# Opening of a fused FFN, attention, FFN kernel: third chunk's sums in two more banks, masks stored a chunk sooner; squares ahead of weights and routing a slot later in the attention phases

## The chip, the cores and the metric

The kernel runs on one core of a Trainium2 chip. The metric is the device time of one execution in microseconds. The core has a matrix engine (TensorE, in the profile PE, with PEld for its weight loads), and VectorE (DVE), ScalarE (ACT) and GpSimd (POOL), which work between the on-chip memory (SBUF) and the accumulators (PSUM, eight banks of 128 x 512 fp32); SyncE (SP) issues DMAs here and computes nothing. ACT and POOL issue DMAs too. Each engine runs its own instructions in the order in which they are written, and they are tied to each other by semaphores.

## The reference, cut to what matters

```python
x = x + 0.5 * ffn(layernorm(x))      # x: 2048 tokens x 512, fp32
x = x + attention(layernorm(x))
x = x + 0.5 * ffn(layernorm(x))

def ffn(x):                          # 64 experts in 8 groups of 8
    scores = softmax(x @ gate_w.T)
    topk_w, topk_idx = top_k(scores, 8)
    w_e = zeros((N, 64)).at[arange(N)[:, None], topk_idx].add(topk_w)
    flat = w_e[:, inv_map]           # N x 8 groups x 8
    scalar = flat.sum(-1)
    soft = softmax(where(flat == 0, -1e9, flat))
    xg = x[:, None] + einsum('ngi,ghi->ngh', soft, mask_up_w)
    g = einsum('ngh,gih->ngi', xg, gate_proj_w)       # i: 352
    u = einsum('ngh,gih->ngi', xg, up_proj_w)
    d = einsum('ngi,ghi->ngh', silu(g) * u, down_proj_w)
    return einsum('ng,ngh->nh', scalar, d)

def attention(x):                    # 4 heads, chunks of 64 tokens
    q, k, v, g = x @ Wq, x @ Wk, x @ Wv, x @ Wg
    gk = log_sigmoid(x @ Wgk1 @ Wgk2 + b) / 16
    o = chunkwise gated linear attention(q, k, v, gk)
    return (rms(o) * Wnorm * silu(g)) @ Wo
```

## The kernel before

**Tiles and phases.** The tokens lie in four blocks of 512. A phase is the FFN of one block, so there are eight phases (`p`), four for each FFN. The 8 x 352 inner columns are cut into 22 chunks of 128 (`CH`; `n = 22 p + i` counts chunks over all phases). For each chunk PE does: the gate sums (`main`, 12 matmuls of 128x512 into a bank, since each fp32 product is three fp32r ones of high and low halves, helper `three`), the mixing matmul that adds the experts' mask part (`soft`, L1380), the same for the up sums, and later the down group of the chunk before (`down(n - 1)`, 12 matmuls into the four banks `YB`, which collect the phase's output). ACT takes silu of the gate bank (L682, `sig`), DVE multiplies by the up bank (L758, `act_t<-bank,sig`) and by the routing scalar (`s_bc`, loaded by ACT, L677), ACT rounds the product (`a_hi`, L509) and DVE subtracts the rest (`a_lo`). `GB`, `UB` are the gate and up bank, `W0`, `W1` two work banks (6 and 7); chunk 1 alone has its gate and up sums in `YB[0]` and `YB[1]`, which are still free.

**Weights.** Phase 0 makes them. SP loads raw weights, ACT casts the high half (`gu_hi`, `d_hi`, L509), DVE subtracts for the low half (`gu_lo`, `d_lo`), PE multiplies the masks with the gate and up weights (`masked(c)`, 8 half-width matmuls L1361, L1362 into `W0`), DVE picks the group's rows (`m_mask`), ACT and DVE round that (`m_top`, `m_rest`), and POOL stores all to DRAM (`store_w`, `store_m`, `store_d`). From phase 1 on SP loads each chunk's weights back: `load_w` (L309, 1152 KB, two buffers `wt`, waits for `u_ok` of two chunks before) and `load_d` (L318, 512 KB, `dt`).

**Slots.** The work between the FFN matmuls is cut into 66 slots for each phase, three for each chunk (`pieces(3 * n)`, `3 * n + 1`, `3 * n + 2`); every engine calls `pieces` at the same places. Phases 1, 2, 4 and 5 (`ATT`) carry the attention of one block each, in slots 13 to 65. All phases but the last carry the routing of the next phase's tokens: statistics, normalization, split of the normalized tokens into `x_hi` (ACT) and `x_lo` (DVE) in `split_slot(p)` and the slot after it, the logits on PE in slot 38 (`router(p, 38)`, L1205, waits for `x_lo_ok`), and the softmax, the top 8 and the transposes in slots up to 51. Before them SP and POOL turn the normalized tokens by quarters with sixteen DMAs of 64 KB (`move_squares`, eight on each queue; SP's are L333); the attention's own tokens are turned likewise at chunk 4 of its phase. In SP's program for chunk 4 the order is `load_w(p, 4)`, `move_squares`, `load_d(p, 3)`.

**The opening.** Ahead of the phase loop PE transposes and routes the first block, does the masks of chunks 0 and 1, the sums of chunks 0 and 1, the transposes of `scal` (L1218) and the eight of `route` (L1224, into `YB[2]` and `YB[3]`, four each). ACT copies these to `softT` (`route_cp`), and only then can the mixing matmuls run. `down(0)` comes in chunk 2's turn, since its banks `YB[0]` and `YB[1]` hold chunk 1's sums until then. ACT issues five DMAs of constants before it casts the weights of chunk 2 (`gu_hi(2)`), and DVE subtracts (`gu_lo(2)`) just before the phase loop.

## Time and profile before

| What | Value |
|---|---|
| Median of three runs | 1832.6 us (1831.39 to 1835.84) |
| The profiled execution | 1832.78 us, of it the span 1831.0 us |
| Mean granted TensorE clock | 0.998 |
| PE busy | 1811.0 us, 99% |
| PEld busy | 1507.7 us, 82% |
| DVE busy | 875.4 us, 48% |
| ACT busy | 512.6 us, 28% |
| POOL busy | 215.6 us, 12% |

How to read the rows. A timeline row has the start in us from the span's start, the duration, the engine, the line, the operation, out<-in, the shapes and how many instructions are taken together; in square brackets stands the engine's idle time just before, and what ended it. "ACTq" and "SPq" are DMA issues on ACT's and SP's queue. A row of a window has its bounds and length, then the busy time and number of instructions of PE, PEld, DVE, ACT, POOL and SP's, then PE's granted clock, the share of the DMA engines and GB/s. A row of DMAs has how many, KB of each, and us from issue to landing. Row numbers of lines are those of the kernel before.

### The profile page before, as it was taken

The numbers are of one execution on the slowest core, as the hardware profiler recorded it, in microseconds if no ns is written. First come the engines' busy times: TensorE is split into PE (matmuls) and PEld (weight loads), VectorE is DVE, ScalarE is ACT, GpSimd is POOL, SyncE is SP. The second block draws the span as 40 slices with busy tenths as digits, with TensorE's granted clock in tenths as the row PEclk, the third lists the DMA queues.
The fourth block names the chain that finished last, engine by engine and source line by source line (L and its number), as shares of the span: only waits on it lengthen the run. The fifth ranks groups of instructions, "written<-read, shape, count | busy, mean of one in ns | idle before, by whom it ended". The sixth has DMA issues, their size and how long they took to land.

```text
span 1831.0 us, 22143 instructions
## 1 busy us (share of the span) xinstructions
PE 1811.0 (99%) x8376; PEld 1507.7 (82%) x8376; DVE 875.4 (48%) x1621; ACT 512.6 (28%) x766; POOL 215.6 (12%) x390
## 2 busy tenths in 40 slices
PE   7999999999999999999999999999999999999999
PEld 5888888888888888888888888888888888888887
DVE  7567454565445663333353656354664334422222
ACT  4334313532125431112212533124432111211111
POOL 1141220011010210010110111010011001000000
PEclk9999999999999999999999999999999999999999
DMA  6987765456365555467756556474456367656664
GB/s 209 363 320 273 276 221 183 157 201 207 125 218 203 168 185 190 166 235 235 246 183 199 192 205 207 139 241 161 154 194 215 134 222 259 226 173 226 236 233 167
DMA packets 103657, 382.04 MB, mean 209 GB/s; under 512 B 16288, under 2 KB 20256, under 8 KB 82816
## 3 DMA queue, kind: packets, MB, share of 16 engines
q1 hardware_dynamic: 58768, 270.50, 42.3%
q0 software_dynamic: 16992, 62.93, 9.3%
q10 hardware_dynamic: 27792, 47.20, 9.2%
q8 instruction: 67, 1.10, 0.2%
q14 instruction: 38, 0.31, 0.1%
HBM read 323.55 MB, written 41.81 MB: 200 GB/s over the span
## 4 chain that ended last, share of the span: by engine, by line
PE 92%; DMA 2%; DVE 2%; issue 1%; ACT 1%; SPq 1%; POOL 0%; ACTq 0%; DVEq 0%; POOLq 0%
PE bank L1176 27%; PE bank L1178 27%; PE bank L1177 27%; PE bank L1380 4%; DMA x_lo<-tb 2%; SPq L333 1%; PE bank L1316 1%; PE bank L1315 1%; PE bank L1361 1%; PE bank L1362 1%; PE bank L1302 1%; PE bank L1308 1%; PE bank L1205 0%; DVE x_lo L758 0%; PE bank L1206 0%
## 5 line engine op out<-in xcount | busy, mean ns | idle before, releaser
L1176 PE MATMUL bank<-x_hi,wt 128*128 128x512 f32 x1328 | 521.2, 393 | 0.0
L1178 PE MATMUL bank<-x_lo,wt 128*128 128x512 f32 x1328 | 517.3, 390 | 0.0
L1177 PE MATMUL bank<-x_hi,wt 128*128 128x512 f32 x1328 | 516.8, 389 | 0.0
L758 DVE TENSOR_TENSOR act_t<-bank,sig 128x512 f32<-128x512 f32 x176 | 121.5, 691 | 512.3 <-PE bank L1380 455.1
L1178 PEld LDWEIGHTS bank<-x_lo,wt 128*128 128x128 f32 x1328 | 249.3, 188 | 52.8
L1177 PEld LDWEIGHTS bank<-x_hi,wt 128*128 128x128 f32 x1328 | 249.5, 188 | 50.7
L1176 PEld LDWEIGHTS bank<-x_hi,wt 128*128 128x128 f32 x1328 | 249.5, 188 | 50.4
L1176 PE MATMUL bank<-dt,a_hi 128*128 128x512 f32 x704 | 277.8, 395 | 0.3 <-DVE a_lo L758 0.3
L1178 PE MATMUL bank<-dt,a_hi 128*128 128x512 f32 x704 | 274.4, 390 | 0.0
L1177 PE MATMUL bank<-dt,a_lo 128*128 128x512 f32 x704 | 274.3, 390 | 0.0
L682 ACT ACTIVATE sig<-bank 128x512 f32<-128x512 f32 x176 | 105.4, 599 | 554.9 <-PE bank L1380 554.8
L509 ACT ACTIVATE a_hi<-act_t 128x512 fp32r<-128x512 f32 x176 | 110.9, 630 | 389.5 <-DVE act_t L758 383.8
L758 DVE TENSOR_TENSOR a_lo<-act_t,a_hi 128x512 fp32r<-128x512 f32 x176 | 121.9, 692 | 118.2 <-ACT a_hi L509 116.8
L1178 PEld LDWEIGHTS bank<-dt,a_hi 128*128 128x128 f32 x704 | 132.2, 188 | 28.4
L1176 PEld LDWEIGHTS bank<-dt,a_hi 128*128 128x128 f32 x704 | 132.3, 188 | 26.7 <-issue 0.7
L1177 PEld LDWEIGHTS bank<-dt,a_lo 128*128 128x128 f32 x704 | 132.3, 188 | 25.9
L1380 PE MATMUL bank<-softT,wt 128*128 128x512 f32 x352 | 134.4, 393 | 1.0 <-ACT softT L509 1.0
L758 DVE TENSOR_TENSOR act_t<-s_bc,act_t 128x512 f32<-128x512 f32 x176 | 129.9, 738 | 7.0 <-DMA s_bc<-scr_s 1.0
L1176 PE MATMUL bank<-x_hi,tw 128*128 128x512 f32 x208 | 81.4, 391 | 0.0
L1177 PE MATMUL bank<-x_hi,tw 128*128 128x512 f32 x208 | 81.4, 391 | 0.0
L1178 PE MATMUL bank<-x_lo,tw 128*128 128x512 f32 x208 | 81.3, 391 | 0.0
L1380 PEld LDWEIGHTS bank<-softT,wt 128*128 128x128 f32 x352 | 66.5, 189 | 15.0 <-issue 1.2
(186 smaller groups left out, 1712.1 us busy)
## 6 DMA issues: line engine op xcount, KB each, us to landing
wt<-scr_w SPq DMA_DIRECT2D x140, 1152.0 KB, 5.2
dt<-scr_d SPq DMA_DIRECT2D x140, 512.0 KB, 5.3
s_bc<-scr_s ACTq DMA_DIRECT2D x128, 256.0 KB, 5.0
state<-wat POOLq DMA_DIRECT2D x28, 512.0 KB, 6.3
scr_w<-wt POOLq DMA_DIRECT2D x12, 1024.0 KB, 8.0
b_all<-wgu SPq DMA_DIRECT2D x22, 512.0 KB, 8.2
scr_d<-dt POOLq DMA_DIRECT2D x22, 512.0 KB, 4.9
scr_w<-tw POOLq DMA_DIRECT2D x10, 1024.0 KB, 7.8
```

The costliest lines, as they stand in the source:

```text
L333: sp.dma_start(turned(s)[cols(j, Q), b, :, :, :], squares[cols(b, Q), j, :, :, :]).then_inc(sq_in[0], 16)
L509: return nc.scalar.activation(dst, src, ACT.Copy)
L682: nc.scalar.activation(sig[:], g_bank(n)[:], ACT.Silu).then_inc(sig_ok, 1)
L758: return nc.vector.tensor_tensor(dst, a, b, op)
L1176: mm(dst, wh, xh, start=start, stop=False)
L1177: mm(dst, wl, xh, start=False, stop=False)
L1178: return mm(dst, wh, xl, start=False, stop=stop)
L1302: ins = mm(W0[:, cols(i)], b_all[:, h, cols(i)], q_all[:, h, cols(i)], start=True, stop=True)
L1308: ins = mm(W0[:, cols(i)], k2t[:, i, :], vtz[:, i, h, :, :], start=True, stop=True)
L1315: mm(W0[:, cols(i)], scm[:, h % 2, i, :], vtz[:, i, h, :, :], start=True, stop=False)
L1316: ins = mm(W0[:, cols(i)], q_all[:, h, cols(i)], state[:, h % 2, 2 * i:2 * i + 2, :], start=False, stop=True)
L1380: return mm(b[:], m[:, c0:c0 + P], softT[:, p % 2, c % 2, :], start=False, stop=True)
```

## The change

**Opening.** `g_bank` and `u_bank` give chunk 2 the banks `YB[2]` and `YB[3]`, and its 24 sums are issued ahead of the phase loop, twelve before and twelve after the transposes of `route`, which go into `W1` and `W0`. `gu_lo(2)` moves from DVE to POOL, and `gu_hi(2)` ahead of ACT's constants' DMAs. Chunks 2 to 4 have their masks made and stored one chunk sooner. PE takes the sums of chunk 3 in chunk 2's turn; `down(0)` and `down(1)` come in chunk 3's turn, `down(2)` and `down(3)` in chunk 4's. The decay weights come a chunk later.

**Squares.** At chunk 4 of the attention phases SP issues `move_squares` ahead of `load_w(p, 4)` instead of behind it.

**Routing.** For phases that follow an attention phase `split_slot` is 37 instead of 36, and every routing step from slot 38 on is done one slot later (`routing_slot`). The split's first half stays ahead of its second by one slot.

The diff, cut:

```diff
@@ banks and slots
-            return YB[0] if n == 1 else GB
+            return YB[2 * n - 2] if n in (1, 2) else GB
-            return YB[1] if n == 1 else UB
+            return YB[2 * n - 1] if n in (1, 2) else UB
-            return 36 if p - 1 in ATT else 33
+            return 37 if p - 1 in ATT else 33
+        def routing_slot(p, k):
+            return k if p == 0 or p - 1 not in ATT or k < 38 else (None if k == 38 else k - 1)
@@ SP
+                    if c == 4 and p in ATT:
+                        move_squares(LN_T[ATT[p]], (p + 1) % 2)
                     if c > 1:
                         load_w(p, c)
-                    if c == 4 and p in ATT:
-                        move_squares(LN_T[ATT[p]], (p + 1) % 2)
@@ POOL
+            def gu_lo(c):
+                pool.wait_ge(gu_hi_ok, c + 1)
+                w = first_w(c)
+                nc.gpsimd.tensor_tensor(w[:, GW:2 * GW], raw_gu[:, c % 2, :], w[:, 0:GW].bitcast(F32),
+                                        ALU.subtract).then_inc(gu_lo_ok, 1)
                 if c + 1 < CH:
                     store_w(c + 1)
-                store_m(c)
+                if c == 0:
+                    gu_lo(2)
+                if c == 0 or c > 4:
+                    store_m(c)
+                if c < 4:
+                    store_m(c + 1)
@@ ACT
+            gu_hi(2)
             act.dma_start(raw_k1, w_gk1).then_inc(ld_const, 16)
...
             act.dma_start(wn[:], wnorm.partition_broadcast(P)).then_inc(ld_const, 16)
-            gu_hi(2)
             gu_hi(3)
                     silu(n)
+                    if n == 2:
+                        gu_hi(4)
                     pieces(3 * n)
                     pieces(3 * n + 1)
                     round_a(n)
-                    if n == 0:
-                        m_top(2)
-                    elif p == 0 and 1 < c < CH - 1:
+                    if n < 3:
+                        m_top(n + 2)
+                    elif p == 0 and 3 < c < CH - 1:
                         m_top(c + 1)
                     if n + 2 < PHASES * CH:
                         load_s(n + 2)
-                    if n == 1:
+                    if n == 2:
                         decay_weights()
                     if p == 0:
                         d_hi(c)
-                        if 0 < c < CH - 3:
+                        if 1 < c < CH - 3:
                             gu_hi(c + 3)
@@ DVE
-            gu_lo(2)
+            dve.wait_ge(gu_lo_ok, 3)
             gu_lo(3)
...
                     gate(n)
-                    if n == 0:
-                        m_mask(2)
-                    elif p == 0 and 1 < c < CH - 1:
+                    if n < 2:
+                        m_mask(n + 2)
+                    elif n == 2:
+                        gu_lo(4)
+                    elif p == 0 and 3 < c < CH - 1:
                         m_mask(c + 1)
                     pieces(3 * n + 1)
                     rest_a(n)
-                    if n == 0:
-                        m_rest(2)
-                    elif p == 0 and 1 < c < CH - 1:
+                    if n == 2:
+                        m_mask(4)
+                    if n < 3:
+                        m_rest(n + 2)
+                    elif p == 0 and 3 < c < CH - 1:
                         m_rest(c + 1)
@@ PE
+                    if i == 0:
+                        pe.wait_ge(scal_cp, 1)
+                    else:
+                        pe.wait_ge(m_raw_ok, 2)
                     for j in range(NT):
-                        ins = nc.tensor.transpose(YB[i + 2][:, cols(j)], route[:, j, cols(i)], ident[:])
+                        ins = nc.tensor.transpose((W1, W0)[i][:, cols(j)], route[:, j, cols(i)], ident[:])
...
             router(0, 46)
+            pe.wait_ge(gu_lo_ok, 3)
+            main(g_bank(2), 0, 0, 2)
             router(0, 49)
             router(0, 50)
+            main(u_bank(2), P, 0, 2)
...
-                    if n > 1:
-                        pe.wait_ge(sig_ok, n if n > 2 else 1)
+                    if n == 2:
+                        loaded(0, 3)
+                        pe.wait_ge(sig_ok, 1)
+                        main(GB, 0, 0, 3)
+                    elif n > 3:
+                        pe.wait_ge(sig_ok, n)
                         main(GB, 0, p, c)
...
-                    if p == 0 and 1 < c < CH - 1:
+                    if n in (1, 2) or p == 0 and 3 < c < CH - 1:
                         masked(c + 1)
-                    if n == 2:
-                        pe.wait_ge(sig_ok, 2)
-                        pe.wait_ge(t1_ok, 2)
+                    if n == 3:
+                        pe.wait_ge(sig_ok, 3)
+                        pe.wait_ge(t1_ok, 3)
                         down(0)
-                    if n > 1:
+                        masked(4)
+                        down(1)
+                    elif n == 4:
+                        down(2)
+                        down(3)
+                    elif n > 4:
                         down(n - 1)
```

How the order moves, at the places that the prediction speaks of. The first is PE in the opening, from the transposes of `scal`; banks 0 to 3 are `YB`, 4 and 5 `GB` and `UB`, 6 and 7 `W0` and `W1`; `tb` holds `route`, and `og` the masks. Before:

```order
L1218 MATMUL bank7<-ident,scal 8x128 [waits scal_ok]
L1218 MATMUL bank7<-ident,scal 8x128 x3
L1224 MATMUL bank2<-ident,tb 128x128 [waits route_ok]
L1224 MATMUL bank2<-ident,tb 128x128 x3
L1224 MATMUL bank3<-ident,tb 128x128 [waits route_ok]
L1224 MATMUL bank3<-ident,tb 128x128 x3
L1380 MATMUL bank4<-softT,wt 128x512 [waits m_ok,route_cp,gu_lo_ok,x_lo_ok]
L1380 MATMUL bank5<-softT,wt 128x512 [waits route_cp,m_ok]
L1380 MATMUL bank0<-softT,wt 128x512 [waits route_cp,m_ok,gu_lo_ok]
L1380 MATMUL bank1<-softT,wt 128x512 [waits route_cp,m_ok]
L1361 MATMUL bank6<-tw,og 128x256 [waits m_raw_ok,gu_lo_ok]
```

Now (twelve sums stand at each place of the first two "..."):

```order
L1243 MATMUL bank7<-ident,scal 8x128 [waits scal_ok]
L1243 MATMUL bank7<-ident,scal 8x128 x3
L1201 MATMUL bank2<-x_hi,tw 128x512 [waits gu_lo_ok]
...
L1254 MATMUL bank7<-ident,tb 128x128 [waits scal_cp,route_ok]
L1254 MATMUL bank7<-ident,tb 128x128 x3
L1254 MATMUL bank6<-ident,tb 128x128 [waits m_raw_ok,route_ok]
L1254 MATMUL bank6<-ident,tb 128x128 x3
L1201 MATMUL bank3<-x_hi,tw 128x512
...
L1413 MATMUL bank4<-softT,wt 128x512 [waits m_ok,route_cp,gu_lo_ok,x_lo_ok]
L1394 MATMUL bank6<-tw,og 128x256 [waits route_cp,m_raw_ok,gu_lo_ok]
```

The sums of chunk 2 stand between the transposes and ahead of the first mixing matmul, and the transposes of `route` are in the work banks.

The second is ACT, from silu of chunk 2 to silu of chunk 3; `b_all` and `k_all` hold raw weights, `gt` a mask product, `state` and `k2t` the constants' raw data. Before:

```order
L682 ACTIVATE sig<-bank4 128x512 [waits t1_ok,g_ok]
L509 ACTIVATE a_hi<-act_t 128x4x4x32 [waits d_used,t2_ok]
L509 ACTIVATE wt<-gt 128x256 [waits st_m1,u_ok,m_raw_ok]
L677 DMA s_bc<-scr_s 96x512
L677 DMA s_bc<-scr_s 32x512
L509 ACTIVATE dt<-k_all 128x512 [waits st_d0,d_used,raw_d_in0]
L509 ACTIVATE wt<-b_all 128x1024 [waits st_w1,u_ok,raw_gu_in1]
L682 ACTIVATE sig<-bank4 128x512 [waits t1_ok,g_ok]
```

Now:

```order
L699 ACTIVATE sig<-bank2 128x512 [waits t1_ok,g_ok]
L525 ACTIVATE wt<-b_all 128x1024 [waits st_w0,u_ok,raw_gu_in0]
L525 ACTIVATE a_hi<-act_t 128x4x4x32 [waits d_used,t2_ok]
L525 ACTIVATE wt<-gt 128x256 [waits st_m0,u_ok,m_raw_ok]
L694 DMA s_bc<-scr_s 96x512
L694 DMA s_bc<-scr_s 32x512
L525 ACTIVATE k1_s<-state 128x16x16 [waits zero_ok,ld_const]
L525 ACTIVATE gk2_s<-k2t 128x512
L525 ACTIVATE dt<-k_all 128x512 [waits st_d0,d_used,raw_d_in0]
L525 ACTIVATE wt<-b_all 128x1024 [waits st_w1,u_ok,raw_gu_in1]
L699 ACTIVATE sig<-bank4 128x512 [waits t1_ok,g_ok]
```

The high half of the weights of chunk 4, the copy of mask 4's product and the constants' copies stand between the two, and the gate sums of chunk 2 are in bank 2.

The third is SP at chunk 4 of phase 1 (the same in phases 2, 4 and 5); `tb` holds the normalized tokens. Before:

```order
L309 DMA wt<-scr_w 128x2304 [waits u_ok]
L333 DMA x_lo<-tb 32x512 [waits sq_ok]
L333 DMA x_lo<-tb 32x512 x7
L318 DMA dt<-scr_d 128x1024 [waits d_used]
L309 DMA wt<-scr_w 128x2304 [waits u_ok]
```

Now:

```order
L322 DMA dt<-scr_d 128x1024 [waits d_used]
L337 DMA x_lo<-tb 32x512 [waits sq_ok]
L337 DMA x_lo<-tb 32x512 x7
L313 DMA wt<-scr_w 128x2304 [waits u_ok]
L322 DMA dt<-scr_d 128x1024 [waits d_used]
```

The eight copies stand ahead of the weights, and the down weights follow both.

The fourth is DVE at the split of the next phase's tokens and the attention's state recurrence, in phase 1; `bank6` holds the state sums of a head. Before:

```order
L758 TENSOR_TENSOR x_lo<-x_lo,x_hi 128x1024 [waits x_hi_ok]
L758 TENSOR_TENSOR act_t<-bank5,sig 128x512 [waits sig_ok,a_lo_ok,u_ok]
L758 TENSOR_TENSOR act_t<-s_bc,act_t 128x512 [waits s_in0,t1_ok]
L758 TENSOR_TENSOR x_lo<-x_lo,x_hi 128x1024 [waits x_hi_ok]
L758 TENSOR_TENSOR a_lo<-act_t,a_hi 128x4x4x32 [waits a_hi_ok,t2_ok]
L954 MEMSET state 128x64 [waits t_lo_ok]
L960 SCALAR_TENSOR_TENSOR state<-state,dec,bank6 128x64 [waits upd_ok,dve_step]
L960 SCALAR_TENSOR_TENSOR state<-state,dec,bank6 128x64 [waits dve_step] x6
L960 SCALAR_TENSOR_TENSOR carry<-state,dec,bank6 128x64 [waits dve_step]
```

Now, from the first of the two subtractions for `x_lo`:

```order
L777 TENSOR_TENSOR x_lo<-x_lo,x_hi 128x1024 [waits x_hi_ok]
L777 TENSOR_TENSOR a_lo<-act_t,a_hi 128x4x4x32 [waits a_hi_ok,t2_ok]
L974 MEMSET state 128x64 [waits t_lo_ok]
L980 SCALAR_TENSOR_TENSOR state<-state,dec,bank6 128x64 [waits upd_ok,dve_step]
L980 SCALAR_TENSOR_TENSOR state<-state,dec,bank6 128x64 [waits dve_step] x6
L980 SCALAR_TENSOR_TENSOR carry<-state,dec,bank6 128x64 [waits dve_step]
L777 TENSOR_TENSOR x_lo<-x_lo,x_hi 128x1024 [waits x_hi_ok]
```

The second subtraction stood ahead of the recurrence of the second head and stands behind it now.

## Rows read from the trace of the kernel before

**Rows 1.** The page, part 1: busy time, share of the span and instructions.
```profile
PE 1811.0 (99%) x8376; PEld 1507.7 (82%) x8376; DVE 875.4 (48%) x1621; ACT 512.6 (28%) x766; POOL 215.6 (12%) x390
```

**Rows 2.** PE's timeline in the opening; then busy time, clock and DMA.
```profile
31.46 0.60 PE L1218 MATMUL bank<-ident,scal 128*8 128x128 f32 x4
33.98 1.09 PE L1224 MATMUL bank<-ident,tb 128*128 128x128 f32 x8 [1.92 <-DVE tb L928]
36.09 2.04 PE L1380 MATMUL bank<-softT,wt 128*128 128x512 f32 x4 [1.01 <-ACT softT L509]
...
36.10:42.10 6.00, 6.00 (x18) 5.13 (x19) 4.18 (x8) 2.87 (x6) 0.00 (x0) 0.50 0.76 194
```

**Rows 3.** Timelines of POOL, DVE and ACT: start, duration, operation, idle before.
```profile
309.69 2.41 POOL L444 TENSOR_TENSOR gt<-gt,wn 128x1024 f32<-128x1024 f32 x1
...
39.31 0.69 DVE L758 TENSOR_TENSOR act_t<-s_bc,act_t 128x512 f32<-128x512 f32 x1 [1.03 <-DMA s_bc<-scr_s]
...
42.55 0.68 DVE L758 TENSOR_TENSOR act_t<-bank,sig 128x512 f32<-128x512 f32 x1
...
25.78 2.01 ACT L509 ACTIVATE tw<-b_all 128x1024 fp32r<-128x1024 f32 x2 [4.37 <-issue]
...
44.53 0.40 ACT L509 ACTIVATE k_s<-state 128x256 fp32r<-128x256 f32 x1
...
46.83 0.57 ACT L682 ACTIVATE sig<-bank 128x512 f32<-128x512 f32 x1
...
51.88 2.01 ACTq L677 DMA_DIRECT2D s_bc<-scr_s  x2
```

**Rows 4.** DVE, PE, SP's queue around copies; then landing times of three loads.
```profile
511.61 0.71 DVE L817 STREAM_TRANSPOSE tb<-o_all 128x512 f32<-128x512 f32 x1
...
521.00 0.39 PE L1176 MATMUL bank<-dt,a_hi 128*128 128x512 f32 x1
...
523.72 0.39 PE L1176 MATMUL bank<-x_hi,wt 128*128 128x512 f32 x1
...
512.58 0.32 SPq L309 DMA_DIRECT2D wt<-scr_w  x1
...
375.51 5.97 SPq L333 DMA_DIRECT2D x_lo<-tb  x8
381.52 0.58 SPq L309 DMA_DIRECT2D wt<-scr_w  x1
...
wt<-scr_w SPq DMA_DIRECT2D x1, 1152.0 KB, 5.1
...
wt<-scr_w SPq DMA_DIRECT2D x1, 1152.0 KB, 7.6
...
wt<-scr_w SPq DMA_DIRECT2D x1, 1152.0 KB, 9.1
```

**Rows 5.** PE's timeline at the attention's first sums, phase 5.
```profile
1228.43 0.50 PE L1176 MATMUL bank<-tw,x_hi 128*128 128x512 f32 x1 [0.72 <-DVE x_lo L758]
```

**Rows 6.** PE and DVE around the logits and the state recurrence; the `x_lo` group.
```profile
389.26 1.05 PE L1308 MATMUL bank<-vtz,k2t 128*128 128x128 f32 x8
390.07 0.48 PE L1205 MATMUL bank<-x_hi,gate_s 128*128 128x512 f32 x1
...
643.40 0.47 PE L1205 MATMUL bank<-x_hi,gate_s 128*128 128x512 f32 x1 [1.31 <-DVE x_lo L758]
...
1342.74 0.47 PE L1205 MATMUL bank<-x_hi,gate_s 128*128 128x512 f32 x1 [2.09 <-DVE x_lo L758]
...
435.22 1.05 PE L1308 MATMUL bank<-vtz,k2t 128*128 128x128 f32 x8
...
436.38 2.18 DVE L960 SCALAR_TENSOR_TENSOR state<-state,dec,bank 128x64 f32<-128x64 f32 x7 [1.42 <-PE bank L1308]
438.59 0.28 DVE L960 SCALAR_TENSOR_TENSOR carry<-state,dec,bank 128x64 f32<-128x64 f32 x1
...
L758 DVE TENSOR_TENSOR x_lo<-x_lo,x_hi 128x1024 fp32r<-128x1024 f32 x22 | 26.9, 1223 | 53.5 <-ACT x_hi L509 53.5
```

More of the change, by code:

```diff
@@ L559, in router @@
                     hi(r, k - split_slot(p), p % 2)
-                elif k == 38:
+                k = routing_slot(p, k)
+                if k == 38:
                     act.wait_ge(logit_ok, p + 1)
@@ L579, in router @@
                     act.wait_ge(routeT_ok, i + 1)
-                    copy(in_order(softT[:, 0, i, :]), by_quarter(YB[i + 2][:].rearrange("p (i b t) -> p i b t", i=NT, b=NQ))).then_inc(route_cp, 1)
+                    copy(in_order(softT[:, 0, i, :]), by_quarter((W1, W0)[i][:].rearrange("p (i b t) -> p i b t", i=NT, b=NQ))).then_inc(route_cp, 1)
             def exps(t, pair):
@@ L862, in router @@
                         turn_squares(r, j)
-                elif k in (split_slot(p), split_slot(p) + 1):
+                elif p and k in (split_slot(p), split_slot(p) + 1):
                     low(r, k - split_slot(p), p % 2)
-                elif k == 39:
+                k = routing_slot(p, k)
+                if k == 39:
                     dve.wait_ge(folded, p + 1)
@@ L1154, in _ @@
                     rest_a(n)
-                    if n == 0:
-                        m_rest(2)
-                    elif p == 0 and 1 < c < CH - 1:
+                    if n == 2:
[3 more added lines that the diff above has]
+                    elif p == 0 and 3 < c < CH - 1:
                         m_rest(c + 1)
-                    if n == 1:
+                    if n == 2:
                         decay_rests()
@@ L1163, in _ @@
                         d_lo(c)
-                        if 0 < c < CH - 3:
+                        if 1 < c < CH - 3:
                             gu_lo(c + 3)
@@ L1192, in router @@
             def router(p, k):
-                r, s = LN_R[p], p % 2
+                r, s, k = LN_R[p], p % 2, routing_slot(p, k)
                 if k == 38:
@@ L1358, in masked @@
                 wait(pe, m_raw_ok, c)
+                if c == 2:
+                    pe.wait_ge(route_cp, 2)
                 hi, lo = weights(0, c)
@@ L1431, in _ @@
                     loaded(p, i)
-                    if n > 1:
-                        pe.wait_ge(sig_ok, n if n > 2 else 1)
+                    if n == 2:
+                        loaded(0, 3)
[3 more added lines that the diff above has]
+                        pe.wait_ge(sig_ok, n)
                         main(GB, 0, p, c)
@@ L1437, in _ @@
                     pieces(3 * n)
-                    if n > 1:
-                        pe.wait_ge(t1_ok, n if n > 2 else 1)
+                    if n > 2:
+                        pe.wait_ge(t1_ok, n if n > 3 else 1)
                         main(UB, P, p, c)
```

3 lines of the change are left out of this document (removed).

## The prediction, made before the changed kernel had run

> **What bounds the kernel now.** The page's busy line comes first: TensorE (PE) is busy 1811.0 us of a span of 1831.0 [rows 1]. The time is PE's matmuls plus PE's holes, and no other engine has half that share. So I read PE's timeline for rows with an idle time in brackets and follow each to its releaser. There are nine in the whole span, and those that the change touches lie in the opening [rows 2], at the attention's first matmul [rows 5] and at the routing's logits [rows 6]. Each edit below is worth the holes that it closes or opens on PE. The profiled execution took 1832.78 us, 1.8 outside the span; the median is 1832.6, and I add the sum to that. The unit of PE's time is the 128x512 matmul, 0.227 us apart at the full clock: a group of 12 takes 2.72 (521.00 to 523.72 in [rows 4]). A shown duration has a modelled tail of 0.16, so a true hole is 0.16 longer than the bracket says.
>
> **Part 1, the opening.** What it can remove [rows 2]: after the four transposes of `scal` (31.46, 0.11 each, to 31.91) PE waits to 33.98, 2.07 us. After the eight of `route` (0.89, to 34.87) it waits to 36.09, 1.22 us. From 36.10 to 42.10 the granted clock is 0.50, the lower level, after those two holes; half of 6.0 us is lost, 3.0. Together **6.3 us**. The change fills the holes with the third chunk's 24 sums. They need its weights split by 31.91. ACT's cast stood behind five DMAs, at 25.78, and moves ahead of them; POOL's subtraction of 128x1024 takes 2.41 us by the only row of that shape [rows 3]. Even at the old place it would end by 25.78 + 1.05 + 2.41 = 29.2, so PE's 31.91 has at least 2.6 us of cover. The first mask stores queue behind it on POOL for under a microsecond; nobody awaits them before the copies of masks 2 and later, 15 us on. SP's load of raw weights 4 waits for this subtraction and now starts several microseconds sooner.
>
> What it adds comes later. PE's new order is 12 sums, 8 transposes, 12 sums, 4 mixing matmuls, masks of chunk 2, 12 sums of chunk 3, 2 mixing, masks of chunk 3, 12 sums, 2 mixing: 31.91 + 2.72 + 0.89 + 2.72 = 38.25 for the first mixing matmul, and 38.25 + 0.91 + 0.97 + 2.72 + 0.45 + 0.97 + 2.72 + 0.45 = 47.4 for the first down group (8 half-width mask matmuls at 0.12 are 0.97). That group overwrites banks that the third chunk's sums now hold, so it waits for DVE's product of chunk 2. DVE's first product starts some 1.2 us after the first mixing matmul, an estimate from silu's 0.57 (46.83) and two hand-overs of 0.3: 39.4. From one product to the next chunk's DVE needs 0.73 + 3.24 (39.31 to 42.55 [rows 3]), twice 3.97: 47.4, ended 48.1. **Wait 0.7 us.** Then down(0) and the masks of chunk 4 end at 51.9, and down(1) at 54.7. PE's next sums overwrite the gate bank that silu of chunk 3 reads. On ACT that silu is queued behind the copy of mask 4, two scale loads, the constants' copies, the down weights and the gate weights of chunk 5. The mask copy can't start before DVE's mask product, some 0.9 us after the masks: 52.8. The two scale loads hold ACT's queue for 2.01 us in the same place before, and the next cast starts 0.4 later; from the constants' first copy to the end of silu it is 2.30 + 0.57 (44.53 to 46.83) [rows 3]. With 0.15 to PE: 58.2. **Wait 3.6 us**; 1.2 if the scale loads issue quickly. Net -6.3 + 0.7 + 3.6 = **-2.0 us**. Bounds: -6.3 (no new wait), +1.0 (the clock falls again in the 3.6 us wait, 3.0 more). It fell in the 4.2 us from 31.91 to 36.09 and held through the wait of 2.09 + 0.16 ahead of 1342.74 [rows 6]; 3.6 lies between, and I take the middle value because full-width matmuls stand on both sides of the new wait, as at 1342.
>
> **Part 2, squares ahead of weights (c = 4 in phases 1, 2, 4, 5).** SP's queue is in order. Now the weights of chunk 4 are issued at 512.58 and the eight copies of squares after them. The transposes end at 512.32 (511.61 + 0.71) and PE starts chunk 4 at 523.72, 11.40 us after them [rows 4]; the other three phases show the same 11.40. After the change the copies start at the transposes' end and take 5.97, as at 375.51 where nothing stands ahead of them, and the weights follow 0.04 later (381.52): 5.39 us ahead of PE. An undisturbed load of 1152 KB landed in 5.1 us (issued 504.0), just in time. Loads issued right behind eight such copies landed in 7.6 (381.52) and 9.1 (1330.8) [rows 4]. The first has the same neighbours, POOL's eight copies beside SP's, so I take it: 7.6 + 0.15 - 5.39 = 2.4 us, four times **9.6**; bounds 0 and 15.6 (9.1). The down weights of chunk 3 are issued at the same time as before. Gained: the squares no longer stand behind 1152 KB, and the attention's first sums no longer wait for them: 0.72 + 0.16 at 1228.43 [rows 5]; in the other three phases the gap is under 0.3 and I count none: **-0.9**. Net **+8.7 us**.
>
> For such a load the Trainium skill ("DMA: Bandwidth & Descriptors", Anatomy of one DMA — SWDGE) gives 2.0 us plus bytes over 436e3, an estimate of 4.7 us. The undisturbed row (5.1) nearly agrees, the rows behind squares (7.6, 9.1) don't; by the page the weights are in time and part 2 is worth -0.9, as in rival (b). The same page's section on queues says that an engine consumes a queue's descriptors in ring order, which speaks against the change: the weights stand behind every copy.
>
> **Part 3, routing a slot later (logits of four phases).** Removed: PE's waits for `x_lo` at 643.40 and 1342.74, 1.31 + 2.09 + 0.32 = **3.7 us** [rows 6]. In the other two phases there is none: the logits (390.07) follow 0.81 after the first state matmul (389.26). Now 12 sums and a mixing matmul come between, 2.95, so PE asks 0.81 + 2.95 = 3.76 us after the first state matmul. But the second `x_lo` subtraction moves one slot as well, and on DVE it then stands behind the state recurrence of the second head, which needs those state matmuls (the order rows). By [rows 6] the recurrence starts 1.16 after the first of them (435.22, 436.38), its last step 2.21 later (438.59) and takes 0.28; the subtraction takes 1.22 and PE hears of it 0.15 later: 5.02. **New wait 1.26 us**, four times 5.0. Net **+1.3 us**; bounds -3.7 (the recurrence is out of the way) and +3 (PE now reaches chunk 13 1.9 us sooner, eight logits matmuls of 0.23, and may find its weights late once or twice). The later routing steps move by the same slot and keep 3 us of matmuls between them; their DVE work meets attention work of other slots, without a matmul that waits for it in the rows.
>
> **Sum:** -2.0 + 8.7 + 1.3 = +8.0; 1832.6 + 8.0 = **1840.6 us**, +0.44%. Edits without a term (masks stored sooner, transposes of `route` into the banks W1 and W0 with a wait for `scal_cp` or `m_raw_ok`, both over before 34.6, constants cast a chunk later) lie beside PE's blocks of 1 to 3 us.
>
> **Rivals.**
> (a) As forecast, the weights late at chunk 4 by 1 to 3.5 us each time: 1835 to 1845. Chance 0.44.
> (b) The weights in time. One mechanism, at the same place: with nothing of SP's left in flight the load lands as the undisturbed one. It decides at 5.24 us. For it: 5.1 at 504.0. Against: both loads behind squares. Then -2.0 - 0.9 + 1.3 = -1.6: 1831.0, not slower. Chance 0.27.
> (c) The change does all that it says: (b), silu of chunk 3 early enough, the recurrence off the path: -6.3 + 0.7 - 0.9 - 3.7 = -10.2: 1822.4. Against it are ACT's and DVE's orders. Chance 0.16.
> (d) Loads at 9.1 and the clock lost in the opening's wait: 1.0 + 15.6 - 0.9 + 1.3 = 17.0: 1849.6, more if the waits at chunk 4 lose it too. For it: 9.1 was seen. Chance 0.13.
>
> A difference under 0.3% (5.5 us) can't be told from none. Faster than 1827.1: (c) and a little of (b), 0.18. Slower than 1838.1: two thirds of (a) and all of (d), 0.44. Between: 0.38. The range leaves out the outer halves of (c) and (d): 1823 to 1848; the likeliest case alone has 1835 to 1845.
>
> **What would show it.** Part 1: PE without a hole from 31.5 to 47.4 at granted clock 1.00, then a short wait before the first down group and some 3 us near 55 released by ACT's silu. Part 2: SP's row of the weights six us behind its first copy, a hole of about 2.4 us ahead of chunk 4 in four phases that ends with the DMA into `wt`, and none at the attention's start. Part 3: four waits of about 1.3 us for `x_lo` ahead of the logits, the subtraction right behind `carry`. The prediction is wrong if those loads land within 5.2 us, if silu of chunk 3 comes before 54.7, or if PE has a hole that none of these rows names.

## The result, and the profile after

The changed kernel takes **1837.87 us** (median of nine executions, 1836.55 to 1840.26) against 1832.6 us for the kernel before (nine executions, 1831.39 to 1836.8). The ratio is 1.0023, with a 95% interval of 1.0015 to 1.0031: 0.23% slower, or 2.7 to 5.7 us. Measured once more on another occasion, as the last experiment below, it was 1836.5 against 1834.93 us, a ratio of 1.0007 (0.9998 to 1.0016). So the change costs some +1 to +5 us by its medians, and the second interval reaches down to none. The forecast was +8.0 (1840.6, 1823 to 1848).

The busy line of the page of the changed kernel, to be held against [rows 1]:

```profile
PE 1812.4 (99%) x8376; PEld 1505.9 (82%) x8376; DVE 873.7 (48%) x1620; ACT 513.6 (28%) x766; POOL 218.1 (12%) x391
```

PE does the same 8376 matmuls; the span grew from 1831.0 to 1838.5 us. The profiled execution took 1840.26 us, the slowest of its nine, and 2.4 us over the median; at least one stretch of half clock that the second trace of this kernel (e12) doesn't have is part of that.

**The opening.** PE's timeline of the changed kernel, at the places of [rows 2], then windows: bounds and length, busy time of PE, PEld, DVE, ACT, POOL, PE's granted clock, DMA share, GB/s.

```profile
34.68 1.04 PE L1254 MATMUL bank<-ident,tb 128*128 128x128 f32 x8
38.29 1.08 PE L1413 MATMUL bank<-softT,wt 128*128 128x512 f32 x4
48.13 0.47 PE L1201 MATMUL bank<-dt,a_hi 128*128 128x512 f32 x1 [0.43 <-issue]
57.90 0.76 PE L1201 MATMUL bank<-x_hi,wt 128*128 128x512 f32 x1 [3.05 <-ACT sig L699]
...
31.82:48.13 16.31, 15.88 (x83) 13.14 (x81) 11.32 (x23) 8.63 (x16) 2.55 (x5) 1.00 0.43 139
57.90:61.35 3.45, 3.45 (x8) 2.74 (x9) 2.65 (x4) 0.63 (x1) 1.59 (x3) 0.52 1.02 360
```

The two holes (idle times of PE) of [rows 2] and the half clock behind them are gone: the first mixing matmul stands at 38.29 where the forecast put it at 38.25, and the first down group starts at 48.13 (forecast 48.1). The new wait is there too, 3.05 us, ended by silu of chunk 3. Behind it the granted clock is 0.52 for 3.45 us, 1.65 us lost, which my sum had only as a bound. From chunk 4 on PE stands 0.44 us ahead of the kernel before, where I had 2.0.

ACT's row of work that silu of chunk 3 stands in, as the order rows of the change have it:

```profile
53.03 0.42 ACT L525 ACTIVATE wt<-gt 128x256 fp32r<-128x256 f32 x1 [1.16 <-DVE gt L777]
53.04 1.68 ACTq L694 DMA_DIRECT2D s_bc<-scr_s  x2
54.82 0.42 ACT L525 ACTIVATE k_s<-state 128x256 fp32r<-128x256 f32 x1 [1.37 <-issue]
...
57.17 0.58 ACT L699 ACTIVATE sig<-bank 128x512 f32<-128x512 f32 x1
```

**Chunk 4 of phases 1, 2, 4 and 5.** PE's timeline, SP's queue in phase 2, and the landing times of the four loads:

```profile
272.38 0.50 PE L1201 MATMUL bank<-x_hi,wt 128*128 128x512 f32 x1 [0.33 <-DMA wt<-scr_w]
526.28 0.50 PE L1201 MATMUL bank<-x_hi,wt 128*128 128x512 f32 x1 [0.44 <-DMA wt<-scr_w]
973.54 0.50 PE L1201 MATMUL bank<-x_hi,wt 128*128 128x512 f32 x1 [1.38 <-DMA wt<-scr_w]
1230.58 0.50 PE L1201 MATMUL bank<-x_hi,wt 128*128 128x512 f32 x1 [1.09 <-DMA wt<-scr_w]
...
514.31 5.01 SPq L337 DMA_DIRECT2D x_lo<-tb  x8
519.37 0.58 SPq L313 DMA_DIRECT2D wt<-scr_w  x1
...
wt<-scr_w SPq DMA_DIRECT2D x1, 1152.0 KB, 6.4
wt<-scr_w SPq DMA_DIRECT2D x1, 1152.0 KB, 6.9
wt<-scr_w SPq DMA_DIRECT2D x1, 1152.0 KB, 7.8
wt<-scr_w SPq DMA_DIRECT2D x1, 1152.0 KB, 7.3
```

The weights are late in all four phases and nowhere by the 2.4 us that the forecast had. The hole at the attention's first sums ([rows 5]) is gone. As counted by PE's position these four places cost 0.62 + 0.34 + 1.25 + 0.37 = 2.6 us.

**The logits.** PE ahead of them in phase 1, and DVE in the same stretch:

```profile
394.91 0.48 PE L1230 MATMUL bank<-x_hi,gate_s 128*128 128x512 f32 x1 [1.44 <-DVE x_lo L777]
...
391.13 2.18 DVE L980 SCALAR_TENSOR_TENSOR state<-state,dec,bank 128x64 f32<-128x64 f32 x7
393.35 0.28 DVE L980 SCALAR_TENSOR_TENSOR carry<-state,dec,bank 128x64 f32<-128x64 f32 x1
393.54 1.22 DVE L777 TENSOR_TENSOR x_lo<-x_lo,x_hi 128x1024 fp32r<-128x1024 f32 x1
```

The subtraction stands right behind `carry` and PE waits for it, here 1.44 us and in phases 2 and 5 1.12 us (forecast 1.26). In phase 4 there is no such wait, since another one comes first on PE: it waits for weights. PE's timeline, SP's queue and the landing of its weights, then the clock behind:

```profile
1093.97 0.50 PE L1201 MATMUL bank<-x_hi,wt 128*128 128x512 f32 x1 [2.30 <-DMA wt<-scr_w]
...
1076.85 6.17 SPq L337 DMA_DIRECT2D x_lo<-tb  x8
1083.19 0.45 SPq L380 DMA_DIRECT2D x_res<-x  x1
1083.69 0.50 SPq L313 DMA_DIRECT2D wt<-scr_w  x1
...
wt<-scr_w SPq DMA_DIRECT2D x1, 1152.0 KB, 10.2
...
1093.97:1098.60 4.63, 4.63 (x14) 3.69 (x15) 1.58 (x3) 0.00 (x0) 0.00 (x0) 0.66 0.80 332
```

These are the weights of chunk 13. SP issues them behind eight copies and behind the load of the last block's tokens (`x_res`, 1024 KB), and they land 10.2 us later. The kernel before had the same three in a row, with the weights issued at 1080.00, and PE started on them at 1089.95, since the eight logits matmuls came first:

```profile
1079.50 0.45 SPq L376 DMA_DIRECT2D x_res<-x  x1
1080.00 0.78 SPq L309 DMA_DIRECT2D wt<-scr_w  x1
...
wt<-scr_w SPq DMA_DIRECT2D x1, 1152.0 KB, 9.3
...
1089.72 0.40 PE L1206 MATMUL bank<-x_lo,gate_s 128*128 128x512 f32 x1
1089.95 0.39 PE L1176 MATMUL bank<-x_hi,wt 128*128 128x512 f32 x1
```

There the margin was 9.95 - 9.3 = 0.65 us, less the hand-over. With the logits a slot later PE comes 1.9 us sooner, which makes 1.25 us of the hole of 2.30; most of the rest is that the same load took 10.2 us here and not 9.3; the clock behind it costs another 4.63 x 0.34 = 1.6.

### The profile page after: what moved, and what is told of

The parts are those of the page before. It is cut to its first block, busy times and chain, and to the rows that moved or that the text cites. A ratio compares the mean times of both kernels' runs of the same rounds, so it can differ in the third digit from the quotient of the medians.

```text
span 1838.5 us, 22142 instructions
## 1 busy us (share of the span) xinstructions
PE 1812.4 (99%) x8376; PEld 1505.9 (82%) x8376; DVE 873.7 (48%) x1620; ACT 513.6 (28%) x766; POOL 218.1 (12%) x391
## 4 chain that ended last, share of the span: by engine, by line
PE 91%; DVE 3%; DMA 2%; SPq 1%; issue 1%; ACT 1%; ACTq 0%; DVEq 0%; POOL 0%; POOLq 0%
PE bank L1201 27%; PE bank L1203 27%; PE bank L1202 27%; PE bank L1413 4%; DMA wt<-scr_w 2%; SPq L337 1%; DVE tb L836 1%; PE bank L1346 1%; PE bank L1345 1%; PE bank L1332 1%; DVE o_all L831 1%; PE bank L1394 1%; PE bank L1395 1%; PE bank L1338 1%; PE bank L1230 1%
```

## The experiments

How far PE stands behind (+) or ahead of (-) the kernel before is read at the start of the down groups, which every kernel has in the same number; the steps between two of them say what a place cost in the profiled execution. The kernel before is one execution too, with 3 us lost to the half clock in its opening and one hole of 0.72 at the attention's first sums in phase 5, so that a kernel with an unchanged opening may show -0.7 to -3.1 there, and -1.0 at that place where it has no hole. All in us:

| Trace | Opening | Chunk 4 in phases 1, 2, 4, 5 | Logits in phases 1, 2, 4, 5 | End |
|---|---|---|---|---|
| changed kernel | -0.4 | +0.6, +0.3, +1.3, +0.4 | +1.8, -0.1, +4.2, -0.9 | +7.1 |
| e12, the same again | +0.7 | +0.7, +0.2, +1.1, -1.0 | +1.8, -0.1, +1.4, -0.9 | +3.8 |
| e1, opening alone | +1.5 | 0, -0.3, 0, -1.0 | 0, +0.1, 0, +1.4 | +1.6 |
| e2, squares alone | -0.7 | +0.1, -0.4, +0.7, -1.0 | 0, +0.2, 0, +2.3 | +1.2 |
| e3, routing alone | -3.1 | +1.0, -0.4, -0.3, -1.0 | +1.8, -0.1, +1.9, -1.0 | -1.2 |
| e4, routing, split at 36 | -2.0 | 0, +0.3, -0.1, -1.0 | 0, -1.5, +2.4, -2.3 | -4.2 |
| e9, opening mended | -5.1 | +1.7, +0.9, -0.1, +0.1 | 0, +0.2, 0, -0.2 | -2.6 |

And the times, each kernel beside runs of the kernel before on the same chip:

| Kernel | Median, us | Before, us | Ratio (95% interval) |
|---|---|---|---|
| e1, opening alone | 1835.66 | 1833.22 | 1.0015 (1.0002 to 1.0028) |
| e2, squares alone | 1833.47 | 1833.22 | 1.0004 (0.9994 to 1.0013) |
| e3, routing alone | 1836.25 | 1833.22 | 1.0016 (1.0004 to 1.0028) |
| e4, routing, split at 36 | 1829.78 | 1833.22 | 0.9979 (0.9971 to 0.9988) |
| e5, e4 and late tokens | 1829.70 | 1833.2 | 0.9981 (0.9972 to 0.9990) |
| e6, opening, sooner silu | 1832.76 | 1833.2 | 1.0004 (0.9995 to 1.0013) |
| e7, e5 + e6 | 1828.66 | 1833.2 | 0.9975 (0.9966 to 0.9985) |
| e8, e7, squares ahead | 1828.37 | 1833.2 | 0.9975 (0.9966 to 0.9984) |
| e9, opening, silu and products sooner | 1830.22 | 1834.69 | 0.9976 (0.9966 to 0.9986) |
| e10, e5 + e9 | 1825.49 | 1834.69 | 0.9955 (0.9942 to 0.9967) |
| e11, e10, squares ahead | 1825.46 | 1834.69 | 0.9950 (0.9938 to 0.9962) |
| e12, changed kernel again | 1836.50 | 1834.93 | 1.0007 (0.9998 to 1.0016) |

### e1: the opening alone

The kernel before with all edits of the opening; the diff is that of the change less these:

```diff
@@ against the changed kernel
-            return 37 if p - 1 in ATT else 33
+            return 36 if p - 1 in ATT else 33
-            return k if p == 0 or p - 1 not in ATT or k < 38 else (None if k == 38 else k - 1)
+            return k
-                    if c == 4 and p in ATT:
-                        move_squares(LN_T[ATT[p]], (p + 1) % 2)
                     if c > 1:
                         load_w(p, c)
+                    if c == 4 and p in ATT:
+                        move_squares(LN_T[ATT[p]], (p + 1) % 2)
```

> The opening's edits alone on the kernel before (squares behind the weights, routing at its old slots). Theory from the two traces: the two holes of 2.07 and 1.22 us and the half clock after them go, and in their place come a short wait before the first down group (0.4), the wait of 3.2 us for silu of chunk 3 and about 1.4 us of half clock behind it: span -0.4 us, a time within 1.5 us of before, granted clock about 0.5 for three to four us from 57.9. Rival: the clock fell after this wait by chance of one execution, and the opening is worth -2.0 us as forecast: the first matmul after the wait then runs at the full clock.

PE's timeline, ACT's rows ahead of it, and the clock behind it:

```profile
58.78 0.77 PE L1201 MATMUL bank<-x_hi,wt 128*128 128x512 f32 x1 [4.15 <-ACT sig L699]
...
53.85 0.42 ACT L525 ACTIVATE wt<-gt 128x256 fp32r<-128x256 f32 x1 [2.21 <-DMA scr_w<-wt]
53.88 1.73 ACTq L694 DMA_DIRECT2D s_bc<-scr_s  x2
...
58.78:65.00 6.22, 6.22 (x16) 4.94 (x17) 4.64 (x6) 2.21 (x3) 2.59 (x5) 0.56 0.89 285
```

The opening alone is not worth -2.0, and not -0.4 either: the ratio is 1.0015. The wait is 4.15 us here and the half clock behind it lasted longer, 6.22 x 0.44 = 2.7 us lost. A cause of the longer wait shows in ACT's row: the copy of mask 4 waited for a DMA `scr_w<-wt`, the store of mask 2, which must have left the buffer. It landed at 53.75 us, 9.1 after its issue. In the changed kernel's first trace it had landed in time, at 52.77 (released by DVE); in its second one (e12) it hadn't, and the wait is 4.08 us. I had said of these stores that they carry no term.

### e2: the squares alone

```diff
+                    if c == 4 and p in ATT:
+                        move_squares(LN_T[ATT[p]], (p + 1) % 2)
                     if c > 1:
                         load_w(p, c)
-                    if c == 4 and p in ATT:
-                        move_squares(LN_T[ATT[p]], (p + 1) % 2)
```

> Only the order of SP's squares and weights at chunk 4 is changed. Theory: the copies take 5.0 to 5.3 us with nothing ahead of them, the weights land 6.4 to 7.8 us after their issue, so PE waits four times 0.3 to 1.6 us there and saves 0.9 at the attention's first sums of phase 5: +2.6 us (1.5 to 4). Rival, the forecast: copies of 5.97 and landings of 7.6, +8.7 us. Second rival: the weights are in time when the opening and the routing are as before, -0.9 us.

The ratio is 1.0004 (0.9994 to 1.0013): no difference that can be told, so neither the 8.7 us of the forecast nor the 2.6 of one trace. The weights landed 5.7, 5.6, 7.2 and 5.8 us after their issue, and PE waited for one load of the four:

```profile
969.96 0.50 PE L1176 MATMUL bank<-x_hi,wt 128*128 128x512 f32 x1 [0.80 <-DMA wt<-scr_w]
```

### e3: the routing alone

```diff
-            return 36 if p - 1 in ATT else 33
+            return 37 if p - 1 in ATT else 33
+        def routing_slot(p, k):
+            return k if p == 0 or p - 1 not in ATT or k < 38 else (None if k == 38 else k - 1)
```

and `k = routing_slot(p, k)` behind the split on ACT and DVE and at the head of `router` on PE.

> Only the routing of the phases behind attention phases is a slot later (split at 37, the rest from slot 38 on). Theory: three or four waits of 1.1 to 1.5 us for x_lo ahead of the logits instead of the two of 1.31 and 2.09, and in phase 4 the weights behind the load of the last block's tokens (issued behind the eight copies there) come late by over 2 us, since PE asks for them 1.9 us sooner; the clock falls behind that wait. Sum +5 us (+3 to +6). Rival, the forecast: only the waits for x_lo, +1.3 us, and the late weights of phase 4 were one execution's, or came from the squares part: no wait for a DMA in phase 4.

```profile
392.63 0.47 PE L1211 MATMUL bank<-x_hi,gate_s 128*128 128x512 f32 x1 [1.44 <-DVE x_lo L763]
645.47 0.48 PE L1211 MATMUL bank<-x_hi,gate_s 128*128 128x512 f32 x1 [1.11 <-DVE x_lo L763]
1088.70 0.50 PE L1182 MATMUL bank<-x_hi,wt 128*128 128x512 f32 x1 [1.58 <-DMA wt<-scr_w]
1344.51 0.47 PE L1211 MATMUL bank<-x_hi,gate_s 128*128 128x512 f32 x1 [1.11 <-DVE x_lo L763]
```

Slower by 0.16% (0.04 to 0.28): the waits for `x_lo` are those of the changed kernel within 0.01 us, and the weights of phase 4's chunk 13 are late without the squares or the opening having been touched. So that wait is the routing's. Its size isn't fixed: 2.30, 1.16 (e12) and 1.58 us.

This profiled execution, at 1831.95 us the fastest of its twelve, shows besides what the clock makes of one and the same stretch. The window after the opening's two holes, of this kernel, and with the same bounds of the kernel before:

```profile
35.72:42.10 6.38, 6.38 (x32) 5.37 (x33) 4.73 (x9) 2.89 (x6) 0.00 (x0) 1.00 0.89 190
...
35.72:42.10 6.38, 6.01 (x18) 5.17 (x19) 4.56 (x8) 3.25 (x7) 0.00 (x0) 0.50 0.73 186
```

The edits of e3 don't touch the opening, and its holes are the same (1.93 and 1.01 in brackets, against 1.92 and 1.01), but the clock stayed at its upper level and 32 matmuls ran where 18 had.

### e4: the split stays at slots 36 and 37

```diff
@@ against e3
-            return 37 if p - 1 in ATT else 33
+            return 36 if p - 1 in ATT else 33
```

> As the one before, but the split of the tokens stays at slots 36 and 37, so that on DVE the second x_lo subtraction stays ahead of the state recurrence; only the logits and what follows are a slot later. Theory: no wait for x_lo ahead of any logits, so some 4.5 us less than with the split at 37; the late weights of phase 4 stay (2.5 us and the clock behind them): -3.4 + 4.2 = about +0.8 us against before. Rival: the waits for x_lo come from ACT's cast or from the copies' landing and not from the place on DVE: then they stay, and the time is that of the kernel with the split at 37.

This is the decisive pair: 1.0016 with the split at 37, 0.9979 with it at 36, some 7 us apart. No wait for `x_lo` ahead of any logits is left on PE, and the late weights are:

```profile
1087.06 0.50 PE L1182 MATMUL bank<-x_hi,wt 128*128 128x512 f32 x1 [2.07 <-DMA wt<-scr_w]
```

So the place on DVE behind the state recurrence was the cause of the waits (three in the trace of e3, of phases 1, 2 and 5). The time is 4 us better than the theory's +0.8. Two things in the traces bear on it, though no run prices them: in this one the clock didn't fall behind the hole of 2.07, and with the holes ahead of the logits the half clock that can follow them goes too (e1 and e2 have it behind theirs in phase 5, 0.67 and 0.70 over 5.2 and 5.6 us).

### e5: the last block's tokens loaded later

```diff
@@ against e4
-                    if p == 4 and c == 12:
+                    if p == 4 and c == 15:
```

> The routing a slot later with the split at 36 and 37 (as before), and besides SP's load of the last block's tokens (1024 KB, x_res) in phase 4 is issued at chunk 15 instead of chunk 12, away from the squares and the weights of chunk 13. Theory: the only hole left on PE near 1087 (2.07 us, ended by the DMA into wt) closes, since the weights behind the eight copies land 1024 KB sooner: 2.2 us less than with the load at 12, 5.6 us less than before. Rival: the weights are late because of the sixteen copies in flight alone; the hole stays at 1 us or more and the time is within 1 us of the one with the load at 12.

The hole at 1087 closed, as the theory has it: with 1024 KB less ahead of them the weights of chunk 13 landed in 7.9 us. But the time is that of e4, 1829.70 against 1829.78, so the 2.2 us didn't come. In this trace they stand elsewhere, at the attention's first sums of phase 4, a place that neither edit touches:

```profile
976.36 0.50 PE L1182 MATMUL bank<-tw,x_hi 128*128 128x512 f32 x1 [1.87 <-DVE x_lo L763]
```

Whether the medians agree for that reason, or because the tokens at chunk 15 hold up other loads, this pair doesn't tell.

### e6: silu of chunk 3 sooner

```diff
@@ against e1, ACT
-                    silu(n)
+                    if n != 3:
+                        silu(n)
                     if n == 2:
                         gu_hi(4)
+                        silu(3)
```

> The opening's edits alone, and ACT issues silu of chunk 3 right behind the cast of the weights of chunk 4, ahead of the copy of mask 4, the scale loads and the constants' copies. Theory: the wait of 3.05 to 4.15 us near 58 is ACT's order alone; it closes, the clock doesn't fall behind it, and the opening is worth -6.3 + 0.6 = about -5 us against before (-3 in an execution of before whose clock did not fall). Rival: PE then waits at the same place for the next thing in the row, DVE's product of chunk 3 or the masks of chunk 4 (2 us or more), and the time stays within 1 us of before.

The rival held. The theory fell: silu now ends before 50, and PE waits half a chunk later, for DVE's product of chunk 3. PE's row, then DVE's:

```profile
60.98 0.80 PE L1203 MATMUL bank<-x_hi,wt 128*128 128x512 f32 x1 [2.38 <-DVE act_t L779]
...
57.35 0.43 DVE L779 TENSOR_TENSOR k_s<-state,k_s 128x256 fp32r<-128x256 f32 x1 [2.35 <-ACT gk_s L525]
57.79 0.68 DVE L779 TENSOR_TENSOR gk_s<-k2t,gk_s 32x512 fp32r<-32x512 f32 x1
58.50 0.69 DVE L779 TENSOR_TENSOR dt<-k_all,dt 128x512 fp32r<-128x512 f32 x1
59.11 1.22 DVE L779 TENSOR_TENSOR wt<-b_all,wt 128x1024 fp32r<-128x1024 f32 x1
60.25 0.68 DVE L779 TENSOR_TENSOR act_t<-bank,sig 128x512 f32<-128x512 f32 x1
```

The product stands on DVE behind four rests, and the first of them waited 2.35 us for ACT, which was at its scale loads. The wait had two owners, one behind the other.

### e7 and e8: both routing edits with e6, squares behind and ahead

> The opening with the sooner silu, the routing a slot later with the split at 36, the late load of the last tokens, and the squares behind the weights as before. Theory: the parts add up, -3.5 to -5 and -5.6: about -9.5 us, 1823.5, with no hole on PE of over 1 us behind 20 us. Rival: what is gained early is lost to other late loads, since PE asks for everything sooner: not under 1828.

> As the one before, with the squares ahead of the weights at chunk 4. Theory: the weights come 0 to 1.4 us late in some of the four phases and the attention's first sums are never late: 0 to +2.5 us against the one with the squares behind. Rival: the order is worth its 0.9 us and the time is lower by that.

0.9975 both, and e7's rival held (not under 1828): the sooner silu without the sooner product adds next to nothing to e5, whose ratio was 0.9981, and the squares' place nothing that can be told. The opening still has its hole for DVE's product, 2.55 us (e7) and 3.11 (e8), so the sum of -9.5 us counted a gain that e6 doesn't have. Behind the weights there are holes for `x_lo` at the attention's first sums (0.97 and 1.58 us), ahead of them holes for `wt` at chunk 4 (0.99, 0.62 and 1.94, the last with the half clock behind it).

### e9: the products of chunk 3 sooner too

```diff
@@ against e6, DVE
-                    gate(n)
+                    if n != 3:
+                        gate(n)
...
                     if n == 2:
+                        gate(3)
                         decay_rests()
```

> The opening alone with the sooner silu, and on DVE the two products of chunk 3 go ahead of the rests of the decay weights, of the down weights of chunk 2 and of the gate weights of chunk 5. Theory: the wait of 2.4 to 3.1 us for DVE's product near 60.5 is those three rests, which themselves wait for ACT behind its two scale loads; with the product at about 55 it closes, the clock doesn't fall in the opening, and the sum is -6.3 + 0.6 = -5.7 us (-3 to -6) against before. Rival: the mask of chunk 5 or the down group of chunk 2 is late next (its weights are rounded behind the same scale loads): a hole of 1 us or more between 55 and 70 stays and the gain is under 3 us.

This closes it. A window of PE from the transposes of `scal` on:

```profile
31.80:64.00 32.20, 31.78 (x160) 26.54 (x159) 22.37 (x38) 15.51 (x27) 6.37 (x12) 1.00 0.70 243
```

32 us with 0.42 us of idle at the full clock; PE stands 5.1 us ahead of the kernel before at chunk 4, and the time is 0.9976 of it (0.9966 to 0.9986), 4.4 us. In its trace 2.5 us of the 5.1 were lost again at the attention's first sums (rows like that of e5 at 274.67, 527.34 and 1226.03 with 1.38, 0.98 and 0.78 us).

### e10 and e11: all of it

e5's routing and e9's opening, with the squares behind (e10) and ahead (e11).

> That opening, the routing a slot later with the split at 36, the late load of the last tokens, the squares behind the weights. Theory: parts add: -3.5 of the routing and -5 of the opening, about -8.5 us, 1824.5 (1822 to 1827), with holes only at the attention's first sums (0 to 1.9 us each). Rival: not under 1828, since the same time is lost at later loads.

> As the one before with the squares ahead of the weights at chunk 4. Theory: same time within 1.5 us: holes of 0 to 2 us for wt ahead of chunk 4 instead of holes of 0 to 1.9 us for x_lo at the attention's first sums. Rival, the forecast's size: 2.4 us late four times, at least 5 us slower than with the squares behind.

**0.9955 and 0.9950**: 8 to 9 us faster than the kernel before, and 10 to 13 faster than the changed one by its two ratios. The parts add up (0.9976 and 0.9981 make 0.9957). The two orders of squares and weights can't be told apart. e11's holes behind 60 us are 0.25, 0.39 and 1.04, all for `wt` at chunk 4, and the 0.34 ahead of the last down group that every trace has; e10 has one in phase 0 that e11 hasn't, 1.51 us at 78.88 for silu, where ACT waited for raw weights. The order isn't its cause: the two kernels differ in SP's program from phase 1 on alone, so that this hole is one execution's.

### e12: the changed kernel again

> The changed kernel once more, for a second trace. Theory: the holes stand at the same places (3 to 4 us at silu of chunk 3, 1.1 to 1.5 for x_lo at three or four of the logits, 1.5 to 2.5 for the weights of phase 4's 13th chunk, 0 to 1.6 at chunk 4 of the four phases), and what differs between the executions is how many of them the half clock follows, 1.5 to 3.5 us each: +4 to +6 us against before, single executions from 1835 to 1841. Rival: the weights late in phase 4 were one execution's, no hole there.

```profile
59.01 0.77 PE L1201 MATMUL bank<-x_hi,wt 128*128 128x512 f32 x1 [4.08 <-ACT sig L699]
1093.71 0.50 PE L1201 MATMUL bank<-x_hi,wt 128*128 128x512 f32 x1 [1.16 <-DMA wt<-scr_w]
...
59.01:62.30 3.29, 3.29 (x8) 2.62 (x9) 2.49 (x4) 0.63 (x1) 1.59 (x3) 0.50 0.86 262
1093.71:1098.60 4.89, 4.89 (x21) 4.05 (x22) 2.59 (x7) 0.60 (x1) 0.00 (x0) 1.00 0.78 317
```

The holes stand at their places, but for the one at chunk 4 of phase 5, whose weights landed in 5.6 us here and 7.3 in the first trace. In phase 4 this one is shorter by 1.1 us and no half clock follows it (21 matmuls in 4.89 us where the first trace has 14 in 4.63); in the opening it is a us longer. The ratio of 1.0007 lies below the theory's range; single executions ran from 1834.64 to 1837.6. The two measurements' intervals meet only at 1.0015 to 1.0016; what differs between them, the chip or the occasion, these runs don't tell.

## Why the prediction came out as it did

**The sign was right, and by the ratio the size was half; both by luck.** The forecast's case (a), weights late at chunk 4 by 1 to 3.5 us each, isn't what happened: two of the four waits were under half a microsecond. The term that made the forecast, +8.7 of +8.0, measured +0.7, and the time came out slower since the two other terms were 4 and 2 us too small. One of the forecast's own signs of being wrong came true as well: the hole of 2.30 us ahead of chunk 13 of phase 4 is none that its rows name, only a bound.

**Part 1, forecast -2.0.** The mechanism is right to a tenth of a us up to 48.13, and the wait for silu was there at the predicted place (3.05 to 4.15 against 3.6). The step that failed is the one on the clock: I argued that full-width matmuls on both sides and one observation (a wait of 2.25 us ahead of 1342.74 that the clock outlived) put this wait on the mild side. It fell in all three traces with this wait (1.7, 2.7 and 1.6 us lost), and the same place in phase 5 that I had leaned on lost it in e1 and e2. The second gap is "masks stored sooner" among the edits without a term: the copy of mask 4 waited for the store of mask 2 in two of three traces, a us each time. The third is the gain: -6.3 took 3.0 us of half clock from one trace, and the four other traces with the opening unchanged (e2 to e5) are 0.7 to 3.1 us faster there, so that there is less to win than I counted. With all three the opening costs +2.4 us by the medians of e1 (ratio 1.0015, 0.4 to 5.1 us), beyond the bound of +1.0, though the interval reaches below it.

**Part 2, forecast +8.7.** Measured alone it is +0.7 us (-1.1 to +2.4). Both halves of the sum were mis-sized. The copies took 5.0 to 5.4 us (e2 and the changed kernel), not 5.97, so the weights were issued 0.8 us sooner. Their landing was 5.6 to 7.2 (e2) or 6.4 to 7.8 us (changed kernel) and not 7.6; I had taken the one row of [rows 4] with the same neighbours as typical. It comes from another place, the routing's copies, where such loads landed in 6.4 to 9.3 us over the traces; at chunk 4 the twenty behind the squares (changed kernel twice, e2, e8, e11) landed in 5.6 to 8.2, around the 6.2 that was left to them, so that the spread decides which are late. Why the two places differ no run shows. And the gain was counted as 0.9 since the trace of before has one hole at the attention's first sums. Other traces with the old order have up to three of them, of 0.27 to 1.87 us: holes of this kind come and go, and one trace samples them. The three errors had the same sign. (In the sum itself 7.6 + 0.15 - 5.39 is 2.36, four times 9.4 and not 9.6.) The rule of the Trainium skill ("DMA: Bandwidth & Descriptors", Anatomy of one DMA — SWDGE) is the page's fit for DMAs of GpSimd's path, and this load is issued by SP; I had used it as if it were for such a load. By it the load takes an estimated 4.7 us and the weights are in time; all eight loads behind the squares of e2 and of the changed kernel landed later than that, at 5.6 us the earliest, so it isn't a time to landing in this queue. Part 2 alone cost about as little as with the weights in time, since in e2 they were issued sooner than I had and three of the four loads made it.

**Part 3, forecast +1.3.** The waits for `x_lo` came as worked out, 1.44, 1.12 and 1.12 against 1.26, and e4 shows the cause by taking them away. The step that failed is a bound that should have been the value: "may find its weights late once or twice", which I priced at up to +1.7 and left out. In phase 4 it happened in every trace with this edit and the tokens loaded at chunk 12 (2.30, 1.16, 1.58 and 2.07 us). The rows to see it in were there: SP's load of `x_res` ahead of those weights, their landing in 9.3 us, and PE's start 9.95 us after their issue. A move of 1.9 us against a margin of 0.65 is not a "may".

**The sum.** e1, e2 and e3 give +2.4, +0.3 and +3.0 us by their medians, +5.7 together, against +5.3 measured at first and +1.6 the second time; by the ratios it is +0.35% against +0.23% and +0.07%. The parts explain the whole, and none is seen to make another worse, but each is known to some 2 us, so that whether they act on each other isn't shown. (A slip beside it: two thirds of (a) and all of (d) make a chance of 0.42, not 0.44.) Rival (d) had the mechanism of the clock; rivals (b) and (c) needed the weights in time and had them in three places of four where the squares were moved alone, and it didn't help, since the routing and the opening cost more than I had.

## What to carry to other kernels

Before work is moved away from in front of a transfer's consumer, take the margin of that transfer (landing against first use) in every place that the move touches; a hole that isn't there yet has no row, but its margin has. A step that is moved a slot on in-order engines comes to stand behind other work on each of them: here one line, the split kept a slot ahead, turned +0.16% into -0.21%. When a wait is removed, look at the next engine's row for the second owner before counting it.

## What the runs showed of the hardware

A hole of the same place and size on PE is followed by the lower clock level in one execution and not in another. The opening's two holes (1.93 and 1.01 in brackets) were followed by a clock of 0.50 for 6.4 us in the kernel before and by none at all in e3; the hole ahead of the logits in phase 5 by 1.00 at 2.09 us (before) and by 0.67 over 5.2 us at 1.98 (e1); the one in phase 4 by 0.66 over 4.6 us at 2.30 and by 1.00 at 2.07 (e4). Each fall cost 1.6 to 3 us, as much as the hole itself, so that a hole of some 2 us is worth between 2 and 4. Executions of one kernel lie 3 to 10 us apart here, and the falls make much of that: of the 34 executions of the kernel before beside e1 to e4, the five with a mean granted clock of 1.000 have a median of 1831.7 us, the eleven with 0.998 one of 1833.9 and the eight with 0.997 or less lie between 1833.0 and 1839.1. The loss of 1.6 us in one fall is 0.001 of that mean.

At chunk 4 a load of 1152 KB behind eight copies of 64 KB landed in 5.6 to 8.2 us over the traces, at the place of the routing of the attention phases in 6.4 to 9.3, and with 1024 KB more ahead of it in 9.1 to 10.3; undisturbed it was 5.1 ([rows 4]). The issue of the eight copies held SP's queue for 5.0 to 5.4 us at chunk 4, and for 5.7 to 6.2 with 1152 KB just ahead (the kernel before and e1).
